# Sixteen-head attention in a two-layer Perceiver kernel: per-head scaling and re-layout of the attended values moved from a TensorE folding product to a GpSimd product and VectorE 32x32 block transposes

## The reference

```python
qh = jnp.einsum('bshd,hed->bshe', q, wq) + bq          # 16 heads of width 16
kh = jnp.einsum('bthd,hed->bthe', kv, wk) + bk
vh = jnp.einsum('bthd,hed->bthe', kv, wv) + bv
scores = jnp.einsum('bshd,bthd->bhst', qh, kh) / jnp.sqrt(jnp.asarray(d, qh.dtype))
attn = jax.nn.softmax(scores, axis=-1)
ctx = jnp.einsum('bhst,bthd->bshd', attn, vh)
out = ctx.reshape(b, sq, e)
return out @ wo.T + bo
```

## Time and profile before

| what | us |
|---|---|
| median of 3 runs | 1461.13 |
| lowest and highest run | 1460.84, 1467.48 |
| span of the profiled execution | 1458.2 |
| TensorE busy | 1389.9 (95%) |
| VectorE busy | 890.9 (61%) |
| ScalarE busy | 834.7 (57%) |
| GpSimd busy | 640.9 (44%) |

### The profile page before, as it was taken

The page is one execution under the profiler, slowest core; times in us unless marked ns, Lnnn a source line. Parts: engine busy times, 40 slices in busy tenths (PEclk is TensorE's granted clock), DMA queues, the critical chain, the costliest instruction groups (busy, mean ns, idle before and its releaser), DMA issues. The chain is left out here.

```text
span 1458.2 us, 51464 instructions
## 1 busy us (share of the span) xinstructions
PE 1389.9 (95%) x19614; PEld 1185.1 (81%) x19647; DVE 890.9 (61%) x3143; ACT 834.7 (57%) x2399; POOL 640.9 (44%) x1195
## 2 busy tenths in 40 slices
PE   8699999999999999999999988999799999999996
PEld 6467878878788878787887766999799999999996
DVE  5678888999999999998999875333111111111111
ACT  1588888888888888888888875331111111111110
POOL 2234444444455454454544543366444444444442
PEclk9999999999999999999999998999899999999999
DMA  9323333333333333333333223666466666666663
GB/s 331 141 71 109 116 97 113 106 109 116 100 104 115 107 118 101 100 119 93 114 97 100 87 87 136 221 181 179 121 181 182 182 181 182 180 185 176 183 182 67
DMA packets 91181, 199.49 MB, mean 137 GB/s; under 512 B 13568, under 2 KB 48128, under 8 KB 79840
## 3 DMA queue, kind: packets, MB, share of 16 engines
q1 hardware_dynamic: 72304, 174.68, 37.5%
q0 software_dynamic: 15680, 18.69, 7.3%
q10 hardware_dynamic: 2992, 3.28, 0.7%
HBM read 178.58 MB, written 18.29 MB: 135 GB/s over the span
## 5 line engine op out<-in xcount | busy, mean ns | idle before, releaser
L2172 ACT ACTIVATE heT<-ps 128x512 f32<-128x512 f32 x142 | 84.7, 597 | 422.9 <-PE ps L2094 397.9
L2094 PEld LDWEIGHTS ps<-xeT,w_block 128*128 128x128 f32 x2272 | 266.5, 193 | 12.8 <-issue 9.5
L2094 PE MATMUL ps<-xeT,w_block 128*128 128x128 f32 x2272 | 268.1, 276 | 8.9 <-DMA w_block<-in_m_w 8.9
L1427 ACT ACTIVATE x_prob<-ps,x_nmax 128x257 f32<-128x257 f32 x512 | 237.7, 474 | 45.2 <-DVE x_nmax L1792 40.2
L2081 PE MATMUL ps<-contexts,heT 128*128 x1136 | 257.6, 379 | 1.6 <-DVE ye L1979 1.6
L2081 PEld LDWEIGHTS ps<-contexts,heT 128*128 128x128 f32 x1136 | 210.1, 190 | 27.6 <-issue 2.0
L1792 DVE TENSOR_REDUCE x_nmax<-ps 128x2 f32<-128x514 f32 x256 | 168.9, 681 | 19.1 <-PE ps L1245 19.1
L1253 PE MATMUL ps<-constants,x_prob 128*128 128x128 f32 x1024 | 152.5, 282 | 10.0 <-ACT x_prob L1427 8.5
L1978 DVE COPY to_ix<-places 128x1 uint32 x71 | 10.9, 154 | 232.0 <-PE ps L2081 228.4
L1431 ACT ACTIVATE x_probT<-ps 128x512 f32<-128x512 f32 x256 | 148.0, 634 | 5.0 <-PE ps L1253 4.7
L2215 POOL TENSOR_TENSOR rt_hold<-constants 128x1 f32<-128x1 f32 x143 | 35.0, 245 | 238.7 <-DVE ye L1979 122.4
(11 more groups left out here) (286 smaller groups left out, 2926.1 us busy)
## 6 DMA issues: line engine op xcount, KB each, us to landing
w_block<-in_m_w SPq DMA_DIRECT2D x71, 1024.0 KB
contexts<-in_cT SPq DMA_DIRECT2D x112, 257.0 KB
contexts<-in_cn SPq DMA_DIRECT2D x112, 256.0 KB
contexts<-in_m_w SPq DMA_DIRECT2D x8, 1024.0 KB
contexts<-in_cT SPq DMA_DIRECT2D x4, 1028.0 KB
xin<-in_x SPq DMA_DIRECT2D x32, 128.0 KB, 2.1
lastq<-in_lastq SPq DMA_DIRECT2D x32, 128.0 KB, 2.3
contexts<-in_cn SPq DMA_DIRECT2D x4, 1024.0 KB
```

The costliest lines, as they stand in the source:

```text
L1427: A(p1[u % 2][:, r, :], ps[:, r, 0:KEYS], ACT.Exp, bias=nmax1[u % 2][:, r:r + 1], accum_out=rsum1[u % 2][:, r:r + 1]).then_inc(e1_ok.handl ...
L2094: t = mm(ps[:, half, at:at + P], w1[b][:, k, f * P:(f + 1) * P], xeT[b][:, k, :], start=k == 0, stop=k == H - 1)
L2172: A(heT[b][:, half * FK // 2:(half + 1) * FK // 2, :].rearrange("p k t -> p (k t)"), ps[:, half, :], ACT.Gelu).then_inc(heT_ok.handle, 1)
```

## The change

- GpSimd's unit_select is replaced by unit_scaled: x_own (64 columns) times x_rinv, broadcast over the 16 columns of a head, into x_scaled. It waits for x_own, for x_rinv and for the transpose of two units before. It stands elsewhere in GpSimd's list.
- VectorE's unit_own loses its second instruction (x_own_half). unit_folded becomes unit_turned, a VectorE transpose of the 32x32 blocks of x_scaled straight into x_outT, at the same places in the list.
- TensorE's unit_fold and its bank waits are gone, in the slots and in the expert stage's opening. The two constants it needed (66 columns) are gone. x1_wv is laid out in another order of heads, so that the blocks land where s1_out wants them.
- Waits that named x_own_half (om_ok) now name x_own (o1_ok): GpSimd's unit_last, the loads of the next context, the expert weights. unit_own and unit_inverse wait for the scaled product of two units before; ff_x waits for x_bias of the tile before; V1 and V3 wait for the next older readers of their banks.

```diff
@@ vector_steps
         def unit_own(t, u):
             q = u % 2
+            before = unit_before(t, u, 2)
             W(dve, v1_ps, t, u + 1)
-            W(dve, sel_ok, t, u + 1)
+            W(dve, lv_ok, t, u + 1)
+            W_if(dve, before[0], n1_ok, before[1] + 1)
             v_.tensor_tensor(own[q][:], bank(B[f"V{u}"])[:, 0:OWN], lastv[q][:], ALU.add).then_inc(o1_ok.handle, 1)
-            W(dve, o1_ok, t, u + 1)
-            v_.tensor_tensor(om[q][:], own[q][:].rearrange("p (r d) -> p r d", r=RG).unsqueeze(1).broadcast_to([P, H, RG, DH]),
-                             select[q][:].unsqueeze(3).broadcast_to([P, H, RG, DH]), ALU.mult).then_inc(om_ok.handle, 1)
-
-        def unit_folded(t, u):
-            W(dve, f1_ps, t, u + 1)
-            v_.tensor_copy(outT[t % 2][:, :, u * S:(u + 1) * S], bank(B[f"f{u}"])[:, 0:HS].rearrange("p (e q) -> p e q", e=HG)).then_inc(f1_ok.handle, 1)
+
+        def unit_turned(t, u):
+            W(dve, n1_ok, t, u + 1)
+            v_.transpose(outT[t % 2][:, :, u * S:(u + 1) * S], scaled[u % 2][:].rearrange("p (j c) -> p j c", j=H)).then_inc(f1_ok.handle, 1)
@@ gpsimd_steps
+        def unit_scaled(t, u):
+            q = u % 2
+            before = unit_before(t, u, 2)
+            W_if(pool, before[0], f1_ok, before[1] + 1)
+            W(pool, r1_ok, t, u + 1)
+            W(pool, o1_ok, t, u + 1)
+            tt(scaled[q][:].rearrange("p (r d) -> p r d", r=RG), own[q][:].rearrange("p (r d) -> p r d", r=RG),
+               rinv1[q][:].unsqueeze(2).broadcast_to([P, RG, DH]), ALU.mult).then_inc(n1_ok.handle, 1)
@@ sync_steps load_w2, and next_batch alike
-            W(sp, om_ok, t, NB)
+            W(sp, o1_ok, t, NB)
@@ TensorE unit_values
                 if u == 1:
-                    W_bank(pe, (t, (f1_ok, 1)))
+                    W_bank(pe, (t + 1, (dve_s["ffn"], "x")), (t - 1, (o1_ok, 3)))
...
                 if u == 3:
-                    W_bank(pe, (t, (f1_ok, 2)))
+                    W_bank(pe, (t + 3, (dve_s["cross0"], "x")), (t, (o1_ok, 1)))
@@ TensorE slot
-                at(s, unit_fold, 0)
...
-                at(s, unit_fold, 1)
                 at(s + 2, ff_up1)
                 at(s + 1, unit_scores, 0)
...
-                at(s, unit_fold, 2)
...
-                at(s, unit_fold, 3)
@@ GpSimd slot
-                at(s + 1, unit_select, 2)
+                at(s + 1, unit_scaled, 1)
                 at(s + 2, q1_blocks)
                 at(s + 1, unit_last, 3)
                 at(s + 4, s0_rstd)
                 at(s + 4, s0_bias)
-                at(s + 1, unit_select, 3)
+                at(s + 1, unit_scaled, 2)
+                at(s + 1, unit_scaled, 3)
                 scatter_behind(s, s + 1, 3)
                 at(s + 2, unit_last, 0)
...
-                at(s + 2, unit_select, 0)
                 at(s + 5, c0_bias)
                 at(s + 2, unit_last, 1)
                 at(s + 1, s1_rstd)
-                at(s + 2, unit_select, 1)
+                at(s + 2, unit_scaled, 0)
                 scatter_behind(s, s + 2, 0)
@@ VectorE
             def ff_x(t):
...
+                W_if(dve, t - 1, bias_s["query1"], "x_bias")
...
             def unit_inverse(t, u):
+                before = unit_before(t, u, 2)
                 W(dve, e1_ok, t, RG * u + RG)
+                W_if(dve, before[0], n1_ok, before[1] + 1)
@@ expert stage, GpSimd (TensorE loses its two unit_fold lines)
+            unit_scaled(tiles - 1, 2)
+            unit_scaled(tiles - 1, 3)
             s1_bias(tiles - 2)
             ro_rstd(tiles - 3)
```

More of the change, by code:

```diff
@@ L46 @@
 MASKED = -1e30
-WIDTH = {"ident": P, "causal": P, "band": P, "half_of_row": H, "head_of_dim": HG, "fold": HS, "before": P,
+WIDTH = {"ident": P, "causal": P, "band": P, "head_of_dim": HG, "before": P,
          "ones": P, "rev8": EXP, "row": 1, "eids": EXP, "column_of": EXP}
@@ L567, in stack_phase @@
     lastv = [sb(f"x1_lastv{q}", [P, OWN]) for q in (0, 1)]
-    select = [sb(f"x1_select{q}", [P, H, RG]) for q in (0, 1)]
     own = [sb(f"x1_own{q}", [P, OWN]) for q in (0, 1)]
-    om = [sb(f"x1_own_half{q}", [P, H, RG, DH]) for q in (0, 1)]
+    scaled = [sb(f"x1_scaled{q}", [P, OWN]) for q in (0, 1)]
     fw = [sb_loop("f1", [P, H, FF], BF16), sb_loop("f2", [P, FK, D], BF16)]
@@ L694, in at @@
         name = step.__name__
-        left = CLOSING.get(name, int(name in ("unit_own", "unit_fold", "unit_folded") and unit[0] >= 2))
+        left = CLOSING.get(name, int(name in ("unit_own", "unit_scaled", "unit_turned") and unit[0] >= 2))
         if 0 <= t < tiles - left:
@@ L793, in ro_logits @@
             product(bank(B["ro_logits"])[:, 0:EXP], [(xnT["router"][:, k, :], router[:, k, :]) for k in range(H)]).then_inc(pe_s["router"].handle, 1)
[L795 removed]
+        return product, product_in_halves, route_counts, W_counts, s1_out, s1_norm_T, s1_q, s1_v_scores, s1_probs_T, s1_values, ro_norm_T, ro_logits
     def vector_steps(dve):
@@ L1083, in setup_folds @@
                 t.then_inc(su_mm, 1)
-            product, product_in_halves, unit_fold, route_counts, W_counts, s1_out, s1_norm_T, s1_q, s1_v_scores, s1_probs_T, s1_values, ro_norm_T, ro_logits = tensor_steps(pe)
+            product, product_in_halves, route_counts, W_counts, s1_out, s1_norm_T, s1_q, s1_v_scores, s1_probs_T, s1_values, ro_norm_T, ro_logits = tensor_steps(pe)
             def c0_norm_T(t):
@@ L2387, in lay_out @@
         d["x1_" + n] = w
-    d["x1_wv"] = d["x1_wv"].reshape(P, H, RG, HG, DH).transpose(0, 1, 3, 2, 4).reshape(P, H, P)
+    d["x1_wv"] = d["x1_wv"].reshape(P, H, H, RG // H, HG, DH).transpose(0, 1, 2, 4, 3, 5).reshape(P, H, P)
     d["router"] = a["L1_ffn_router_w"].T
```

57 lines of the change are left out of this document (18 added, 39 removed), and 4 rows, old and new, of the table B.

## The result

The changed kernel takes 1468.9 us (median of 20 runs, 1464.4 to 1472.5), the kernel before, run between them, 1461.9 (20 runs, 1456.6 to 1467.5). The ratio is 1.0047, 95% interval 1.0035 to 1.0059: 7 us slower, where 3 us faster was forecast.

The account below looks back on a forecast made before the run. A cycle of waits across engines, period 26.07 us, was taken as the bound. Steady tiles 0, last tiles 2 and expert opening 0.7 made about 3 us less than 1461.1: 1458 us, range 1450 to 1468.

Parts of the forecast that it names:

- Bound and steady tiles: Stack stage: the 26.07 us period is a cycle of waits, not one engine's sum; the change gains 0 in steady tiles.
- Holding of ffn_rounded and ffn_xq: VectorE, stretch from unit 3's scores to unit 0's maximum: GpSimd's query_blocks products hold both, so own_half's 0.32 us is spent.
- the 0.63 us becoming 1.27: VectorE's idle time before self_masked, waiting for ScalarE's self_val: would grow from 0.63 to about 1.1 us.
- the transpose at 0.234: VectorE's 32x32 block transpose replacing the fold copy: 0.25 us taken, up to about 0.4 would cost nothing.
- GpSimd's shift: GpSimd's table writes, x_bias and self_x_bias come 0.3 us later, 0.8 in a group's first tile; neutral for VectorE's ffn_hidden.
- the rule of turns: End of the stack stage: x_bias, ffn_hidden, self_x_bias and ffn_hq alternate between GpSimd and VectorE, each holding the other once.
- Rival R3: GpSimd wins twice, x_bias holding ffn_hidden and self_x_bias ffn_hq: 0.7 us in 18 scattering tiles, 12.6 less 3, 1470; chance 0.09.
- its own sign: In tiles with scatters, ffn_hq over 1.1 us and unit 1's exponentials 0.7 later would show GpSimd winning twice.
- The folds as cover: TensorE's 128 folding products, 46.1 us: removal counted at nothing in steady tiles, since work behind them waits anyway.
- The last tiles and the expert stage: s1_values' waits for unit 3's fold copy go, 1 us in each of two tiles; two folds leave the expert opening, 0.7.

Follow-up runs that it names:

- the additions ahead: GpSimd's x_bias and self_x_bias moved from behind last 0 to right behind self_0's bias: kernel before 1453.9 us (ratio 0.9936), changed kernel 1449.6 us (0.9909).

## Why the prediction was wrong, step by step

- **Bound and steady tiles: right.** A cycle, not TensorE's 95%: without the folds' 46.1 us tiles 2 to 4 took 78.14 and 78.09 us, where they had taken 78.10. Holding of ffn_rounded and ffn_xq, the 0.63 us becoming 1.27 (about 1.1 was said), and the transpose at 0.234 (0.25 was taken) came as worked out.
- **GpSimd's shift: the step that failed.** It was called neutral: "in turn, each holds the other once". Two errors. The size, 0.3, counted the products' own time; the table writes came 1 us later and 0.54 was left of it. And the rule of turns was read from one row, where VectorE had asked first and GpSimd waited. In nine of the 14 tiles 12 to 25 x_bias was running when ffn_hidden asked, self_x_bias followed it before VectorE got in, and ffn_hidden took 1.81 us instead of 1.26. Turn-taking came true only in tiles 12, 16, 20 and 24. Rival R3 had GpSimd winning twice in a row and nearly the price (0.7 a tile; 0.55 for the hold, 0.72 with the cast), with a chance of 0.09. It was not right in all: it put the second hold on ffn_hq and counted 18 tiles, but both holds fell on ffn_hidden, ffn_hq kept its 0.69, and its own sign (ffn_hq over 1.1) didn't come. That its 9.6 us (12.6 less 3) lies near the 7 measured is in part luck, since the 7 hold TensorE's stalls and the clock in tile 0 as well.
- **cross_x_bias was not counted.** It stood behind unit_select 0, whose wait kept it late; with that gone it rose by 1 to 3 us and met ffn_hq in tile 1 (0.42) and the cast in table-writing tiles (0.16). A step that is removed also frees what stood behind it in its queue.
- **The folds as cover.** "At nothing" held for time, not for TensorE's clock: in tile 0 the wait grew from 0.92 to 1.18 and the clock fell, 1.35 us, which was not in the sum. In one of the seven traces without folds (the changed kernel with the additions ahead) the same 1.18 us left the clock at full speed and the tile at 25.32.
- **The last tiles and the expert stage: right in the waits and for the expert stage, the 2 us of the last tiles not shown.** s1_values, in the earlier trace rows 1.10 us late for the fold's copy, in the changed kernel (order of time, TensorE, two tiles):

```profile
876.18 0.70 PE L765 MATMUL ps<-self_val,self_probT 128*128 128x256 f32 x2 [0.37 <-ACT self_probT L878]
...
901.71 0.70 PE L765 MATMUL ps<-self_val,self_probT 128*128 128x256 f32 x2 [0.37 <-ACT self_probT L878]
```

It waits for ScalarE 0.37. The closing of the stack took 59.2, 60.3 and 55.9 us in the three traces with folds, 55.7 to 58.9 (mean 56.6) in the seven without. The means are 1.8 apart where 2 were said, but the ranges overlap, and with the additions ahead in both kernels the closings are 55.86 and 55.70: the 2 us are not told apart from nothing. The expert stage is shorter by 0.5 and 0.9 in the two traces of the changed kernel, 0.7 were said. With the additions ahead in both, the changed kernel is the faster by 4.3 us, about the forecast's 3, but not by the forecast's terms: tiles 12 to 25 take 366.54 with folds and 362.46 without, a typical one 25.9 and 25.7. By an estimate from that, 14 x 0.2 = 2.8 of the 4.1 us are the folds' place in steady tiles, which the forecast put at nothing, as it is in the order of the kernel before.

The Trainium skill (SBUF — State Buffer, section Who interferes with whom) says that the port pair shared by VectorE and GpSimd goes, where a VectorE instruction runs in a two-port mode, to whichever instruction issues first, for all of it, and that tensor_reduce never contends on trn2. The maximum's 1.28 us beside x_bias agrees. The order doesn't in tile 15: ffn_hidden asked at 497.37, self_x_bias at 497.89, and self_x_bias went first; by the page's rule ffn_hidden would have ended at 497.95 + 0.56 = 498.51, not 499.18, and self_x_bias would have met ffn_hq instead, as my forecast had it. In tile 16 the order agrees: ffn_hidden asked at 526.55, self_x_bias at 526.68, and ffn_hidden went first.

## What to carry to other kernels

- Where a queue gets a new wait, follow every instruction behind it to the engine that it can hold, not only to the one that waits for it: an engine at 44% busy set most of 7 us here. Putting the expected delay alone into the old kernel tests that without the change.
- Before an engine's work is moved off the path, look at who holds the path's longest SBUF instruction: two additions moved ahead by 4 to 5 us gave 0.6% in the kernel before and 1.3% in the changed one.
- Removing work from an engine can cost: its cover for the clock, the place of what stood behind it, and the places of its stalls change. Compare stages by period before comparing whole times.
- A rule read from one row doesn't justify a term of nothing: look for the same meeting of instructions in other tiles. Tile 20 of the kernel before already shows it otherwise. ffn_hidden asks under x_bias and ends behind self_x_bias:

```profile
622.55 0.74 POOL L914 TENSOR_TENSOR x_bias<-x,r_x_bo 128x256 f32<-128x256 f32 x1
623.17 1.40 DVE L1755 TENSOR_SCALAR ffn_hidden<-ffn_hidden,ffn_qscale 128x1024 f32<-128x1024 f32 x1
623.24 0.73 POOL L914 TENSOR_TENSOR self_x_bias<-x,r_a_bv 128x256 f32<-128x256 f32 x1
```

## What the runs showed of the hardware that I had not expected

- A VectorE instruction that waits under one GpSimd product was also overtaken by the next: 1.81 us where 1.26 is one hold and 0.74 none. Between the two query_blocks products VectorE does get in (ffn_rounded ends 0.17 behind the first), and in tile 16 of the changed kernel between the same two additions (ffn_hidden 0.77, self_x_bias 1.22). What decides between the two cases was not settled.
- TensorE's product of one column in fp32 costs 254 ns, of 64 columns 262.
- TensorE stalls of 0.5 to 2.2 us with no releaser in the trace, in tiles that mostly repeat between traces of one program and change with the program. Behind one of 1.90 us the clock was granted at 0.50 (1.2 GHz), behind one of 1.74 us it stayed at full speed.
